# A sixteen-batch two-layer transformer block: the rows for the second layer's experts written before the second head group's copy and turned later, and VectorE's loop closed before the second normalisation

## The chip, the cores and the metric

The kernel runs on one core of a Trainium2 chip. The metric is the device time of one execution in microseconds. Before the change it was 1889.29 us, the median of 3 runs (1885.23 to 1890.84).

## What is computed

The input is 16 sequences of 512 tokens with 128 features. Four residual steps follow, the first three behind a layer normalisation without weights:

```
x = x + attention_0(layernorm(x))   # 16 heads of 8; q and k scaled to length 1; no softmax; (k'v) first
x = x + experts_0(layernorm(x))     # 8 experts, top 2 by softmax score, and 2 shared ones; silu(x w1) * (x w3) @ w2
x = x + attention_1(layernorm(x))   # 16 heads of 8, softmax with a causal band mask
x = x + experts_1(layernorm(x))     # 16 experts; each takes the 512 tokens with the highest logits, gelu between two layers
```

For the last line a token is normalised once more inside the experts' layer: `xn = xf / rms(xf) * norm_weight`, the router's logits are `xn @ router_weight.T + router_bias`, and each expert gathers the rows `xn[idx]` that it takes. So each batch has to leave behind, besides its x, its 512 normalised rows (called `row` in the kernel) and their logits. The experts themselves run after the sixteenth batch.

## The kernel before, in words

**Stages of a batch.** The kernel keeps several batches in flight. Each batch passes a front stage f (first attention, first experts), a stage r (q, k and v of the second attention, split into bf16 parts and sent through DRAM into the tiles `QT` and `KT`), a stage b (the second attention's scores, row maxima, exponentials and products) and a tail stage t (output projection, x3, `row`, router). Work alternates between two phases, written once and run by all engines in the same order, each engine with its own instruction queue:

- `x_phase(f, b, t, g)`: the first experts of batch f (ten units: `up`, `up3`, `product`, `down`), beside them the scores by query of batch b, whose row maxima VectorE takes (`maxima`), and the start of batch g;
- `y_phase(b, f, r, t)`: the scores by key of batch b, whose exponentials ScalarE takes (`exps`), the products with v in four head groups (`outputs(0)` to `outputs(3)`), beside them the first attention of batch f (`f_kvq`, `f_kv`, `f_kvo`, `f_out`, `f_turn_x1`, `f_gate`), stage r of another batch, and the tail of batch t.

The order inside a phase is written out by hand for each engine. Engines meet only through semaphores. `looped` (line 268) runs five phases as straight code, then a loop over i from 1 to BATCH - 3 with an x_phase and a y_phase in its body, then six more phases as straight code. TensorE, ScalarE and POOL close their loop between a y_phase and the next x_phase.

**The scores.** A batch has 40 fills (`scores`) of three PSUM banks `ba`, in each phase once. In a y_phase fill n waits for exponential n - 3, and `outputs(k)` (line 834) waits for exponentials 0 to 10k + 9 and, for k > 0, for the normalisation `norm(k - 1)`. Each head group goes the same way: `outputs(k)` on TensorE into the bank `bo`, a copy `oT<-bo` on VectorE (also called `outputs`, line 1377), `turn_outputs(k)` on TensorE back into `bo` (line 743), `norm(k)` on VectorE (lines 1269 and 1271: a reciprocal `rden`, and the product into `ao`). Only then may the next group's products be written to `bo`.

**VectorE in a y_phase.** The order before the change is: `r_norm`, `f_bias`, `r_center`, `f_bias`, `f_l2`, `r_rest`, `f_scale`, `outputs(0)`, `r_rest`, `t_stats`, `norm(0)`, `f_kvm`, `t_square`, `outputs(1)`, `t_row`, `norm(1)`, `f_x1`, `outputs(2)`, `t_logits`. Then follow, in a second part called with `rest=True`, `norm(2)`, `f_logits`, `f_gates`, `f_rank` and `outputs(3)`. VectorE's loop is closed between the two parts: its body is the rest of a y_phase, an x_phase, and the first part of the next y_phase. `fc`, `mc`, `rc` and `tc` are counters of the steps of one batch; `fc.b` tells the counter which batch it is in.

**The rows of the second experts.** `t_stats` takes mean and variance of x3; POOL raises to the power -0.5 (`power`, line 452, `t_rs`); `t_square` makes from it the variance of the normalised rows (`t_ve`), POOL takes a second power (`t_rs2`); `t_row` multiplies the two (`t_sc`, line 1300) and writes `row` with four instructions (line 1146). TensorE's `t_turn_row` turns `row` into `facc` (line 729, four transposes), ScalarE copies that with the norm's weight into `rowT` (line 1043), and TensorE's `t_router` (line 735) makes the logits, which VectorE's `t_logits` stores (line 1307). SyncE sends `row` to DRAM (`row_dmas`, line 347), behind the transfers of the next `QT` and `KT` of the first eight heads.

**The front's side.** `f_kvo` (line 642) makes k'v times the output weights in `fa[1]`, ScalarE copies it into `kvo` behind exponential 24, `f_out` (line 648) makes the attention's output, and `f_x1` on VectorE (from line 1209) adds it to x, takes the statistics, waits for a power of POOL (`f_rs`) and writes `f_n`, which `f_turn_x1` turns (line 609).

Of the kernel before, what the change touches and what calls it, by code (L numbers as in the profile page):

```python
# [20 lines left out]
BATCH, SEQ, D = 16, 512, 128  # L21
# [24 lines left out]
def build_kernel(nc, a, out):  # L46
    ctx = ExitStack()
    with ctx:
# [557 lines left out]
        def _(pe):  # L606
# [202 lines left out]
            def y_phase(b, f, r, t):  # L809
                def fills(*ns):  # L810
                    if b is None:
                        return
                    for n in ns:
                        if n == 0:
                            pe.wait_ge(S["s_mx0"], 16 * PARTS * (b + 1))
                            pe.wait_ge(S["s_red"], FILLS * (b + 1))
                        if n == FILLS // 2:
                            pe.wait_ge(S["s_mx1"], 16 * PARTS * (b + 1))
                        if n >= 3:
                            pe.wait_ge(S["s_exp"], FILLS * b + n - 2)  # L820
                        scores(pe, b, n, True)

                def outputs(k, *beside):
                    if b is None:
                        return
                    pe.wait_ge(S["s_exp"], FILLS * b + 10 * k + 10)
                    if k == 0:
                        pe.wait_ge(S["s_nmT"], 2 * b + 2)
                    else:
                        pe.wait_ge(S["s_norm"], 4 * b + k)  # L830

                    for blk in range(Q):
                        for j in range(4):
                            last = pe.matmul(bo[32 * j:32 * j + 32, blk * P:], lhsT=vp[:, blk, 4 * k + j],  # L834
                                             rhs=prob_block(4 * k + j, blk), start=blk == 0, stop=blk == Q - 1)
                        if blk == Q - 1:
                            last.then_inc(S["s_pv"], 1)
                        fills(*beside[blk:blk + 1])

                def if_b(step, *args):  # L840
                    if b is not None:
                        step(b, *args)

                def if_f(step, *args):
                    if f is not None:
                        step(f, *args)

                def if_r(step):
                    if r is not None:
                        step(r)  # L850

                def if_t(step, *args):
                    if t is not None:
                        step(t, *args)

                if_f(f_kvq, 0)
                fills(0, 1, 2)
                if_f(f_kvq, 1)
                fills(3, 4)
                if_b(turn_maxima, 1)  # L860
                if_r(r_turn)
                fills(5, 6, 7)
                if_r(r_q)
                fills(8, 9, 10, 11)
                outputs(0, 12, 13, 14)
                if_r(r_k)
                fills(15, 16, 17)
                if_b(turn_outputs, 0)
                fills(18, 19)
                if_f(f_kv)  # L870
                fills(20, 21)
                outputs(1, 22, 23, 24)
                if_f(f_kvo)
                if_t(t_turn_row, r)
                fills(25, 26, 27)
                if_b(turn_outputs, 1)
                fills(28, 29)
                if_f(f_out)
                fills(30, 31)
                outputs(2, 32, 33, 34)  # L880
                if_t(t_router)
                fills(35, 36)
                if_f(f_turn_x1)
                fills(37)
                if_b(turn_outputs, 2)
                fills(38, 39)
                if_f(f_gate)
                if r is not None:
                    if t is not None:
                        pe.wait_ge(S["s_l1c"], t + 1)  # L890
                    r_v(r)
                outputs(3)
# [73 lines left out]
        def _(act):  # L966
# [37 lines left out]
            def y_phase(b, f, r, t):  # L1004
                def exps(first, last):
                    if b is None:
                        return
                    for n in range(first, last + 1):
                        pair, f_ = divmod(n, 5)
                        act.wait_ge(S["s_st"], FILLS * b + n + 1)  # L1010
                        if f_ == 0:
                            act.wait_ge(S["s_pv"], 4 * b + max(pair - 1, 0) // 2)
                        act.activation(probs[:, pair % 3, f_], ba[n % 3][:], ACT.Exp, scale=SCALE).then_inc(S["s_exp"], 1)  # L1013

                if b is not None:
                    act.activation(warm[:], m_b[:, 0:1], ACT.Exp, scale=0.0)
                exps(0, 4)
                if b is not None:
                    copy(nmT[:, 1], bo[:].bitcast(BF16)[0:PARTS * HEADS // 2, 0:SEQ], "s_nmt", 2 * b + 2, "s_nmT")
                if r is not None:  # L1020
                    copy(b_nT[:], facc[:], "s_T3", r + 1, "s_nT3")
                exps(5, 5)
                if f is not None:
                    act.wait_ge(S["s_kvqe"], Q * f + Q)
                    act.activation(sq[:].rearrange("p q (w d) -> p q w d", w=2), kvq[:].rearrange("p q (w d) -> p q w d", w=3)[:, :, 0:3:2],
                                   ACT.Square).then_inc(S["s_sq"], 1)
                exps(6, 7)
                if r is not None:
                    act.wait_ge(S["s_qkw"], 48 * r)
                    copy(qkp[:, 0, 0], facc[:], "s_q", r + 1, "s_p1")  # L1030
                exps(8, 14)
                if r is not None:
                    copy(qkp[:, 1, 0], facc[:], "s_k", r + 1, "s_p1")
                exps(15, 19)
                if f is not None:
                    copy(qnT[:], fa[0][:], "s_qT", f + 1, "s_qnT")
                exps(20, 24)
                if f is not None:
                    copy(kvo[:], fa[1][:, 0:D], "s_kvo", f + 1, "s_kvoc")
                exps(25, 26)  # L1040
                if t is not None:
                    act.wait_ge(S["s_T4"], t + 1)
                    act.activation(rowT[:], facc[:], ACT.Copy, scale=norm_col[:]).then_inc(S["s_nT4"], 1)
                exps(27, 36)
                if f is not None:
                    copy(f_nT[:], fa[0][:], "s_T2", f + 1, "s_nT2")
                exps(37, 39)
                if f is not None:
                    act.wait_ge(S["s_lgx"], f + 1)
                    act.activation(sc[:], lg[:], ACT.Exp).then_inc(S["s_exf"], 1)  # L1050
                if r is not None:
                    act.wait_ge(S["s_pv"], 4 * r)
                    copy(vp[:, :, :, 0:HD], facc[:].rearrange("p (q h d) -> p q h d", q=Q, h=HEADS), "s_v", r + 1, "s_vp")
# [41 lines left out]
        def _(dve):  # L1095
# [283 lines left out]
            def y_phase(b, f, r, t, rest=False):  # L1379
                def if_b(step, k):  # L1380
                    if b is not None:
                        step(b, k)

                def if_f(step, *w):
                    if f is not None:
                        step(f, *w)
# [5 lines left out]
                def if_t(step):  # L1392
                    if t is not None:
                        step(t)

                if rest:
                    fc.b = f
                    if_b(norm, 2)
                    if_f(f_logits)
                    if_f(f_gates)  # L1400
                    if_f(f_rank)
                    if_b(outputs, 3)
                    return
# [10 lines left out]
                if_b(norm, 0)  # L1414
                if_f(f_kvm)
                if_t(t_square)
                if_b(outputs, 1)
                if_t(t_row)
                if_b(norm, 1)
                if_f(f_x1)  # L1420
                if_b(outputs, 2)
                if_t(t_logits)

            def y_whole(b, f, r, t):
                y_phase(b, f, r, t)
                y_phase(b, f, r, t, True)
# [3 lines left out]
            x_phase(0, None, None, 1)  # L1430
            y_whole(None, 1, 0, None)
            x_phase(1, 0, None, 2)
            y_phase(0, 2, 1, None)
            with dve.Fori(1, BATCH - 2) as i:
                y_phase(i - 1, i + 1, i, i - 2, True)
                x_phase(i + 1, i, i - 1, i + 2)
                y_phase(i, i + 2, i + 1, i - 1)
# [221 lines left out]
```

## Time and profile before

| | |
|---|---|
| median of 3 runs | 1889.29 us (1885.23 to 1890.84) |
| the profiled execution: its time | 1888.15 us |
| its span in the profile | 1885.8 us |
| mean granted clock of TensorE over the span | 0.907 |
| first and last turn of `row` | 268.13 and 1522.9 us |
| passes of VectorE's loop | 13 |
| after the batches: choice of tokens and the sixteen experts | from about 1527 us |

The profile is one execution. Times are microseconds from the start of the span. PE is TensorE's matmuls, PEld its weight loads, DVE VectorE, ACT ScalarE, POOL GpSimd, SP SyncE. A timeline's line gives the start, the time from the first start to the last end of the merged instructions, the engine, the line of the kernel, the operation with its output and inputs, the number of instructions and, in square brackets, how long the engine sat idle before it and what released it. "Issue" as a releaser says that the engine waited for nothing that the profile shows. The granted clock of TensorE has two levels, 1.00 (2.4 GHz) and 0.50 (1.2 GHz); a number in between is the mean of a stretch that has both.

### The profile page before, as it was taken

To read this page: it belongs to the slowest core of one execution; us is meant where nothing else is said; L and a number is where in the kernel's file an instruction comes from. 1 tells how busy PE (TensorE), PEld (TensorE's weight loads), DVE (VectorE), ACT (ScalarE), POOL (GpSimd) and SP (SyncE) were. 2 spreads that over 40 slices of the span, in tenths; PEclk is the share of its full clock that TensorE was granted. 3 is DMA by queue.
4 is the path that set the end of the run, shared out by engine and by line. 5 is a ranking of instruction groups with operands and counts; after the bars stand their busy time and mean duration, and the time that the engine had idled before them with its cause. 6 is when DMAs were issued, how large, how long until landed. Compare 5 with 4: busy or idle time off the path is not lost.

```text
span 1885.8 us, 35247 instructions
## 1 busy us (share of the span) xinstructions
PE 1558.1 (83%) x10840; PEld 974.4 (52%) x10840; DVE 1217.5 (65%) x3591; ACT 862.5 (46%) x1787; POOL 518.3 (27%) x498
## 2 busy tenths in 40 slices
PE   2889989999999999998989898999998821356765
PEld 2455656565655555565656565656564411244654
DVE  5567868686868686867777686868675358821110
ACT  1436464645555554545464646464553412423331
POOL 1322222131313131312222222213121020038886
PEclk7879999999999999999999999999999765578897
DMA  2031121303030303031221212130303000034443
GB/s 70 1 79 47 40 64 29 73 18 85 7 84 7 84 15 81 24 67 39 52 54 37 54 37 58 33 77 14 79 8 84 8 12 0 1 73 95 91 85 60
DMA packets 83244, 90.77 MB, mean 48 GB/s; under 512 B 19520, under 2 KB 73024, under 8 KB 78528
## 3 DMA queue, kind: packets, MB, share of 16 engines
q1 hardware_dynamic: 71872, 80.76, 17.5%
q0 software_dynamic: 11264, 8.92, 3.5%
q14 instruction: 84, 0.69, 0.1%
q8 instruction: 24, 0.39, 0.1%
HBM read 58.95 MB, written 29.92 MB: 47 GB/s over the span
## 4 chain that ended last, share of the span: by engine, by line
PE 52%; DVE 18%; issue 15%; POOL 6%; DMA 3%; ACT 3%; SPq 1%; DVEq 1%; POOLq 0%; ACTq 0%
PE fa L675 7%; PE ba L585 6%; PE ba L580 6%; PE fa L667 6%; PE bo L834 5%; PE fa L685 4%; POOL out L552 3%; PE ba L587 2%; PE facc L685 2%; PE ba L953 2%; DVE passed L1488 2%; PE ba L582 2%; DVE nm L1258 2%; DMA QT<-nmT 2%; POOL got L522 2%
## 5 line engine op out<-in xcount | busy, mean ns | idle before, releaser
L1013 ACT ACTIVATE probs<-ba 128x512 f32<-128x512 f32 x640 | 352.3, 598 | 191.9 <-PE ba L582 190.7
L458 POOL TENSOR_TENSOR x<-x,gd 128x512 f32<-128x512 f32 x144 | 182.5, 1267 | 615.4 <-ACT gd L991 598.1
L580 PE MATMUL ba<-QT,KT 75*128 75x512 bf16 (+3 forms) x1024 | 262.2, 319 | 27.7 <-ACT probs L1013 14.5
L585 PE MATMUL ba<-KT,QT 72*128 72x512 bf16 (+3 forms) x1024 | 244.2, 305 | 7.4 <-DVE nm L1258 3.2
L580 PEld LDWEIGHTS ba<-QT,KT 75*128 75x128 bf16 x1024 | 106.7, 104 | 188.0 <-ACT probs L1013 104.1
L582 PE MATMUL ba<-mask_k,identb 128*128 128x128 bf16 x1024 | 200.2, 229 | 0.0
L1258 DVE TENSOR_REDUCE nm<-ba 128x1 f32<-128x512 f32 x256 | 174.3, 681 | 36.0 <-PE ba L587 36.0
L587 PE MATMUL ba<-mask_q,identb 128*128 128x128 bf16 x1024 | 192.9, 222 | 0.0
L834 PE MATMUL bo<-probs,vp 128*32 128x512 f32 (+3 forms) x2048 | 182.2, 445 | 1.7 <-ACT probs L1013 0.9
L675 PE MATMUL fa<-f_nT,w 128*128 128x512 f32 x320 | 174.3, 627 | 2.5 <-DVE hh L1250 1.5
L667 PE MATMUL fa<-f_nT,w 128*128 128x512 f32 x320 | 173.8, 625 | 0.0
L585 PEld LDWEIGHTS ba<-KT,QT 72*128 72x128 bf16 x1024 | 101.2, 99 | 99.6 <-issue 37.6
L1260 DVE TENSOR_REDUCE nm<-ba 128x1 f32<-128x384 f32 x256 | 140.3, 548 | 16.6 <-PE ba L587 16.6
L991 ACT ACTIVATE gd<-facc,gates 128x128 f32<-128x128 f32 x256 | 73.2, 369 | 131.0 <-PE facc L685 131.0
L984 ACT ACTIVATE sil<-fa 128x512 f32<-128x512 f32 x160 | 95.3, 596 | 76.9 <-PE fa L667 76.9
L587 PEld LDWEIGHTS ba<-mask_q,identb 128*128 128x128 bf16 x1024 | 101.8, 99 | 55.1 <-issue 53.6
L1250 DVE TENSOR_TENSOR hh<-sil,fa 128x512 f32<-128x512 f32 x160 | 108.6, 678 | 15.5 <-PE fa L685 8.8
L991 ACT ACTIVATE gd<-fa,gates 128x128 f32<-128x128 f32 x256 | 73.2, 369 | 92.4 <-PE fa L685 92.4
L582 PEld LDWEIGHTS ba<-mask_k,identb 128*128 128x128 bf16 x1024 | 105.8, 103 | 15.6 <-issue 13.1
L552 POOL DMA_INDIRECT out<-contrib,cur x64 | 100.7, 1574 | 30.8 <-issue 18.6
L1596 DVE TENSOR_TENSOR ysum<-ba,fb 128x512 f32<-128x512 f32 x16 | 11.1, 691 | 151.6 <-PE ba L953 151.6
L1377 DVE COPY oT<-bo 128x512 f32<-128x512 f32 x64 | 44.1, 690 | 88.2 <-PE bo L834 88.2
(279 smaller groups left out, 2785.1 us busy)
## 6 DMA issues: line engine op xcount, KB each, us to landing
QT<-qk_parts SPq DMA_DIRECT2D x96, 192.0 KB
KT<-qk_parts SPq DMA_DIRECT2D x96, 192.0 KB
qk_parts<-qkp SPq DMA_DIRECT2D x32, 384.0 KB, 2.5
fc<-in_L_ffn_fc_weight SPq DMA_DIRECT2D x32, 256.0 KB, 3.1
xin<-in_L_attn_x SPq DMA_DIRECT2D x16, 256.0 KB, 7.8
qk_parts<-qkp SPq DMA_DIRECT2D x16, 256.0 KB, 2.7
out<-x SPq DMA_DIRECT2D x16, 256.0 KB, 2.3
xn_rows<-row SPq DMA_DIRECT2D x16, 256.0 KB, 6.6
```

Source lines behind the costliest of these rows:

```text
L458: pool.tensor_tensor(x1[:], x1[:], gd[:, e % 2], ALU.add).then_inc(S["s_x1g"], 1)
L552: pool.indirect_dma_start(out_rows, bass.IndirectOffsetOnAxis(cur[k][:, c:c + 1], 0), contrib[k % 2][:, c], None, compute_op=ALU.add).then ...
L580: pe.matmul(bank[:, col:col + w], lhsT=KT[0:K_ROWS, head, blk * P:(blk + 1) * P], rhs=QT[0:K_ROWS, head, blk * P:], start=True, stop=False)
L582: last = pe.matmul(bank[:, col:col + P], lhsT=identb[:], rhs=mask_k[:], start=False, stop=True)
L585: pe.matmul(bank[:, col:col + w], lhsT=QT[0:QK_ROWS, head, blk * P:(blk + 1) * P], rhs=KT[0:QK_ROWS, head, 0:w], start=True, stop=False)
L587: last = pe.matmul(bank[:, col + w - P:col + w], lhsT=identb[:], rhs=mask_q[:], start=False, stop=True)
L667: pe.matmul(fa[0][:], lhsT=w1[:, e], rhs=f_nT[:], start=True, stop=True).then_inc(S["s_h1"], 1)
L675: pe.matmul(fa[1][:], lhsT=w3[:, e], rhs=f_nT[:], start=True, stop=True).then_inc(S["s_h3"], 1)
L834: last = pe.matmul(bo[32 * j:32 * j + 32, blk * P:], lhsT=vp[:, blk, 4 * k + j], rhs=prob_block(4 * k + j, blk), start=blk == 0, stop=blk ...
L991: last = act.activation(gd[:, e % 2, q], down_bank(e - 2)[:, q * D:(q + 1) * D], ACT.Copy, scale=gates[:, q, e - 2:e - 1])
L1013: act.activation(probs[:, pair % 3, f_], ba[n % 3][:], ACT.Exp, scale=SCALE).then_inc(S["s_exp"], 1)
L1258: last = dve.tensor_reduce(nm[:, 3, h:h + 1], bank[:], X, ALU.max, negate=True)
```

## The change

On TensorE `t_turn_row` moves from behind `f_kvo` to behind fill 29; `f_out` moves from behind fill 29 to behind fill 28. On ScalarE the copy `rowT` moves from behind exponential 26 to behind exponential 29. On VectorE `t_row` moves ahead of `outputs(1)`, and the loop is closed behind `outputs(1)`: `norm(1)`, `f_x1`, `outputs(2)` and `t_logits` go to the part that begins the loop's body. Since that part now has a tail step, which has no batch in the loop's first pass, this pass is written out ahead of the loop, and VectorE's loop runs from 2.

```
@@ TensorE, y_phase
                 if_f(f_kvo)
-                if_t(t_turn_row, r)
                 fills(25, 26, 27)
                 if_b(turn_outputs, 1)
-                fills(28, 29)
+                fills(28)
                 if_f(f_out)
+                fills(29)
+                if_t(t_turn_row, r)
                 fills(30, 31)
                 outputs(2, 32, 33, 34)
                 if_t(t_router)
@@ ScalarE, y_phase
-                exps(25, 26)
+                exps(25, 29)
                 if t is not None:
                     act.wait_ge(S["s_T4"], t + 1)
                     act.activation(rowT[:], facc[:], ACT.Copy, scale=norm_col[:]).then_inc(S["s_nT4"], 1)
-                exps(27, 36)
+                exps(30, 36)
@@ VectorE, y_phase
                 if rest:
                     fc.b = f
+                    if_b(norm, 1)
+                    if_f(f_x1)
+                    if_b(outputs, 2)
+                    if_t(t_logits)
                     if_b(norm, 2)
                     if_f(f_logits)
                     if_f(f_gates)
...
                 if_t(t_square)
+                if_t(t_row)
                 if_b(outputs, 1)
-                if_t(t_row)
-                if_b(norm, 1)
-                if_f(f_x1)
-                if_b(outputs, 2)
-                if_t(t_logits)
@@ VectorE, the phases
             x_phase(1, 0, None, 2)
-            y_phase(0, 2, 1, None)
-            with dve.Fori(1, BATCH - 2) as i:
+            y_whole(0, 2, 1, None)
+            x_phase(2, 1, 0, 3)
+            y_phase(1, 3, 2, 0)
+            with dve.Fori(2, BATCH - 2) as i:
                 y_phase(i - 1, i + 1, i, i - 2, True)
                 x_phase(i + 1, i, i - 1, i + 2)
                 y_phase(i, i + 2, i + 1, i - 1)
```

## Rows read from the trace of the kernel before

**Rows 1.** The page: busy time by engine, and the chain that ended last.

```profile
PE 1558.1 (83%) x10840; PEld 974.4 (52%) x10840; DVE 1217.5 (65%) x3591; ACT 862.5 (46%) x1787; POOL 518.3 (27%) x498
...
PE 52%; DVE 18%; issue 15%; POOL 6%; DMA 3%; ACT 3%; SPq 1%; DVEq 1%; POOLq 0%; ACTq 0%
```

**Rows 2.** The list of waits, 600 to 950: us in total, times, longest.

```profile
PE facc L729 <- DVE row L1146: 7.4, 4, 1.8
...
PE bo L743 <- DVE oT L1377: 3.4, 8, 0.6
```

**Rows 3.** Timeline of PE, one y_phase of the loop.

```profile
265.80 0.49 PE L642 MATMUL fa<-w_o,kvm 128*128 128x128 f32 x2
268.13 0.65 PE L729 MATMUL facc<-ident,row 128*128 128x128 f32 x4 [1.84 <-DVE row L1146]
...
270.66 1.11 PE L648 MATMUL fa<-kvo,qnT 128*128 128x128 f32 x8
271.61 0.38 PE L580 MATMUL ba<-QT,KT 75*128 75x512 bf16 x1
...
272.35 1.06 PE L834 MATMUL bo<-probs,vp 128*32 128x512 f32 x8
...
277.85 0.60 PE L609 MATMUL fa<-ident,f_n 128*128 128x128 f32 x4
...
287.07 0.65 PE L743 MATMUL bo<-ident,oT 128*128 128x128 f32 x4 [0.54 <-DVE oT L1377]
```

**Rows 4.** Timeline of DVE, the same y_phase.

```profile
262.77 0.17 DVE L1296 TENSOR_SCALAR t_ve<-t_ve 128x4 f32<-128x4 f32 x1
265.93 0.69 DVE L1377 COPY oT<-bo 128x512 f32<-128x512 f32 x1 [3.00 <-PE bo L834]
...
266.89 1.11 DVE L1146 TENSOR_SCALAR row<-x,t_mv,t_sc 128x128 f32 x4 [0.19 <-DVE t_sc L1300]
...
271.81 0.69 DVE L1209 TENSOR_TENSOR x<-fa,xres 128x512 f32<-128x512 f32 x1 [1.07 <-PE fa L648]
...
275.36 1.11 DVE L1146 TENSOR_SCALAR f_n<-x,f_mv,f_rs 128x128 f32<-128x128 f32 x4 [1.12 <-POOL f_rs L452]
```

**Rows 5.** Timeline of POOL, the same y_phase: the second power.

```profile
263.02 1.01 POOL L452 TENSOR_TENSOR t_rs<-t_ve,mhalf 128x4 f32<-128x4 f32 x1 [0.82 <-DVE t_ve L1296]
```

**Rows 6.** Windows: busy PE, PEld, DVE, ACT, POOL (instructions); PEclk, DMA share, GB/s.

```profile
266.00:281.00 15.00, 13.16 (x126) 9.03 (x126) 6.64 (x25) 9.37 (x19) 1.01 (x1) 1.00 0.42 95
...
712.00:714.00 2.00, 0.51 (x6) 0.30 (x2) 1.65 (x6) 0.65 (x2) 0.00 (x0) 1.00 0.75 197
714.00:721.00 7.00, 6.65 (x33) 5.46 (x34) 0.77 (x3) 3.42 (x6) 0.00 (x0) 0.51 0.71 150
721.00:728.00 7.00, 7.00 (x71) 3.70 (x70) 4.10 (x16) 3.80 (x7) 1.01 (x1) 1.00 0.00 1
```

**Rows 7.** Line 729 on PE: starts of later turns, and idle before all.

```profile
356.02 1.11 PE L729 MATMUL facc<-ident,row 128*128 128x128 f32 x4 [1.83 <-DVE row L1146]
...
1341.85 0.85 PE L729 MATMUL facc<-ident,row 128*128 128x128 f32 x4 [1.84 <-DVE row L1146]
...
DVE row L1146: 35.0, 16
```

**Rows 8.** Line 1269 (norm) on DVE: behind the loop's end, and over all.

```profile
280.85 0.26 DVE L1269 RECIPROCAL rden<-bo 128x16 f32<-128x16 f32 x1 [3.09 <-issue]
...
L1269 DVE RECIPROCAL rden<-bo x64: 242/256/259, 175.4 to 1512.9; 128x16 f32<-128x16 f32 x64
...
issue: 34.5, 12
```

**Rows 9.** Timeline of ACT, the same y_phase: the exponentials behind `kvo`.

```profile
269.17 1.09 ACT L1013 ACTIVATE probs<-ba 128x512 f32<-128x512 f32 x2 [2.57 <-PE ba L582]
```

**Rows 10.** DMA by queue: 726.5 to 730, then 730 to 732: packets, MB, share.

```profile
q14 instruction: 1, 0.01, 0.8%
...
q14 instruction: 1, 0.01, 3.1%
```

More of the change, by code:

```diff
@@ L873, in y_phase @@
                 if_f(f_kvo)
-                if_t(t_turn_row, r)
                 fills(25, 26, 27)
                 if_b(turn_outputs, 1)
-                fills(28, 29)
+                fills(28)
                 if_f(f_out)
+                fills(29)
+                if_t(t_turn_row, r)
                 fills(30, 31)
@@ L1039, in y_phase @@
                     copy(kvo[:], fa[1][:, 0:D], "s_kvo", f + 1, "s_kvoc")
-                exps(25, 26)
+                exps(25, 29)
                 if t is not None:
@@ L1043, in y_phase @@
                     act.activation(rowT[:], facc[:], ACT.Copy, scale=norm_col[:]).then_inc(S["s_nT4"], 1)
-                exps(27, 36)
+                exps(30, 36)
                 if f is not None:
@@ L1397, in y_phase @@
                     fc.b = f
+                    if_b(norm, 1)
+                    if_f(f_x1)
+                    if_b(outputs, 2)
+                    if_t(t_logits)
                     if_b(norm, 2)
@@ L1416, in y_phase @@
                 if_t(t_square)
+                if_t(t_row)
                 if_b(outputs, 1)
[L1418 to L1422, printed above, removed]
             def y_whole(b, f, r, t):
@@ L1432, in _ @@
             x_phase(1, 0, None, 2)
-            y_phase(0, 2, 1, None)
-            with dve.Fori(1, BATCH - 2) as i:
+            y_whole(0, 2, 1, None)
+            x_phase(2, 1, 0, 3)
+            y_phase(1, 3, 2, 0)
+            with dve.Fori(2, BATCH - 2) as i:
                 y_phase(i - 1, i + 1, i, i - 2, True)
```

## Prediction, made before the change was run

> **What bounds the kernel now.** I read the busy shares first [rows 1]: TensorE is busy 83% of the span, VectorE 65%, ScalarE 46%, and the chain that ended last is 52% TensorE. So up to about 1,527 us, while the batches pass, time is gained only where TensorE idles or runs slowly. The list of waits over four passes of the loop says where it idles on VectorE: 1.8 us per pass before line 729, the turn of `row`, and 3.4 us in 8 times, 0.6 at most, before line 743, the turns of the outputs [rows 2].
>
> The reader is then to look at one second phase (y_phase) at full clock [rows 3]. TensorE starts `f_kvo` at 265.80 and then idles 1.84 us before the turn of `row` at 268.13; nothing else of the group waits. On VectorE [rows 4] the last thing that `t_row` needs from its own engine, `t_ve`, is done at 262.94, and POOL's power on it took 1.01 us from 263.02 [rows 5]. Then VectorE stands 3.00 us, because `outputs(1)`, the copy of the second head group, is ahead of `t_row` in its queue and waits for TensorE's line 834. Only after that copy come `t_sc` and the four writes of `row`, to 268.00. The stall is made by the order of two steps, not by missing data.
>
> The stall has a second price. From 712 to 714 TensorE worked 0.51 us of 2; from 714 to 721 the granted clock was 0.51, the lower of its two levels (1.2 of 2.4 GHz), and before and after it was 1.00 [rows 6]. The pass of 268 has the same stall and stays at 1.00 [rows 6]. Every later pass of the loop falls, each right behind the stall and nowhere else (windows of 2 us over the loop, of which the group shows one pass). The starts of line 729 price it [rows 7]: from 268.13 to 356.02 is 87.89 us with no fall between; the eleven intervals from 356.02 to 1341.85 last 985.83 us, against 11 x 87.89 = 966.79. So eleven falls cost 19.0 us.
>
> Third, the end of VectorE's loop. Behind `logits` it starts nothing until 280.85, 3.09 us put down to issue; over all passes it is 34.5 us in 12 times, 2.9 each [rows 8]. Behind it `lg`, the gates and the fourth copy are late, and TensorE waits 0.54 us for that copy at 287.07 [rows 3]. Of the 3.4 us of [rows 2], one wait of 0.56 per pass is the first copy's; 3.4 - 4 x 0.56 = 1.2 in four passes, 0.3 each, lies behind the loop end.
>
> **Part 1: `t_row` ahead of `outputs(1)` on VectorE.** Power done at 264.03, `t_sc` at about 264.3, the wait of 0.19 or so and four writes of 1.11 in all: `row` is ready at about 265.7. VectorE was idle there for 3.00 us [rows 4], which hides all of it. The copy starts at 265.93 as before, with a margin of 0.2 us; if a power came late the copy would slip, but TensorE's turn of it comes only after three more score fills, 0.9 us on. SyncE's one DMA of `row` becomes free to leave 2.3 us sooner; it still stands behind the QT/KT transfers in the queue, has the same size, and nothing in the pass reads it: nothing.
>
> **Part 2: the turn moved on TensorE, behind fills 25 to 29 and `f_out`.** The same instructions follow without the hole: what lies between 268.13 and `outputs(2)` at 272.35 [rows 3] is 4.22 us of work and starts at 268.13 - 1.84 = 266.29, so `outputs(2)` starts at 270.5. `f_out` moves ahead of the turn (at most 0.65) and of fill 29 (0.36): it was done at 271.61, 3.48 us after 268.13, and is now at 266.29 + 3.48 - 0.85 = 268.9. ScalarE must keep up: its next exponential came 2.57 us late because of the stall [rows 9]. Now five exponentials at some 0.52 (1.09 for two [rows 9]) from 266.6 end by 269.9 even with gaps, ahead of 270.5 where `outputs(2)` wants them. The `rowT` copy behind them ends near 270.6, and `t_router` comes only after `outputs(2)`. Its move costs nothing.
> Thirteen passes x 1.84 = 23.9 us. The idle before line 729 is 35.0 us in 16 times [rows 7], so the last three turns have 35.0 - 23.9 = 11.1. The very last has no head groups beside it and keeps its wait, the most of these; the other two are like the loop's, though with less work of other stages between the fills, so ScalarE limits sooner. I take 1.6 each, 3.2.
>
> **Part 3: the clock.** With no hole TensorE works on, and the nearest stretch without this stall, 721 to 728 with the same kind of head-group products, has clock 1.00 [rows 6]. The holes of up to 0.6 us before line 743 never brought a fall. So the low stretches go: 19.0 us for eleven and as much again for one, 1.3, behind the stall of 1341.85: 20.3. Bounds: 0, if something else there makes it fall, and 20.3.
>
> **Part 4: the loop end.** Its old place becomes plain code: `norm(2)` and `lg` follow TensorE, and the 0.3 us at the fourth copy goes, 12 x 0.3 = 3.6. Bounds 0 and 12 x 0.54 = 6.5; I take 3.6.
> At the new place, behind the second copy (ends at 266.62 [rows 4]), 2.9 us reach to 269.5; `norm(1)` takes 0.6 and is done at 270.1; `outputs(2)` wants it at 270.5: a margin of 0.4 us, 0.3 with the semaphore's way. `f_x1`, queued behind it, finds `f_out` ready since 268.9. Its chain took 271.81 to 276.47, 4.66 us with POOL's power in it [rows 4], and now ends at 274.8; TensorE wants `f_n` at 277.85 - 272.35 = 5.5 us behind `outputs(2)`'s start [rows 3], at 276.0: a margin of 1.2.
> So the cover is thin and the length of this end decides. It has a fetch in it: in the old, quiet place the one packet of the instruction queue took 0.8% of 16 engines x 3.5 us = 0.45 us; between 730 and 732, in other traffic, one took 3.1% of 16 x 2 us = 1.0 us [rows 10]. The new place lies in traffic, 0.71 to 0.75 of the DMA engines' time [rows 6]. Bounds for the added length: 0 (the same length) and 2 us (this fetch and a following one, each doubled, and queueing); I take the difference of the two packets, 0.55, of which 0.25 shows on TensorE. Eleven ends are left: 2.8 us lost.
> The Trainium skill (Runtime: NRT & Kernel Launch, Instruction fetch mechanics) says that a taken branch to a target outside what the engine holds must wait for a DMA fetch of it. By that rule the end lasts as long as a transfer does and speaks against this new place; the packet inside the gap agrees.
> The peeled pass is straight code; `norm` shows an issue gap only 12 times in 64 [rows 8], one for each loop end, none in the straight passes: nothing.
>
> **The sum.** 23.9 + 3.2 + 20.3 + 3.6 - 2.8 = 48.2 us. The profiled execution took 1888.15 us, 1.1 below the median of 1889.29 of the runs shown; 1888.15 - 48.2 = 1840. Its own range is 1832 (the two upper bounds of part 4 and of the last turns, and some 3 us of low clock in the last passes that may shift) to 1848.
>
> **The rivals.**
> - The stall goes, the clock falls all the same. Against it: no fall anywhere else in the loop. For it: the stretch ahead of the hole is 128x32 products, little work per matmul, and `f_kvo` is small. Then 20.3 stays: 1860. Chance 0.12.
> - The loop end stretches in its new place to 4 to 5 us. At 4.5 `norm(1)` is 1.3 late beyond the margin: 11 x (1.3 - 0.25) = 12, so 1852; were that hole to bring the falls of [rows 7] again, 1866. Chance 0.12.
> - Slower than before, at the same place: VectorE between the second copy and `norm(1)`, with `outputs(2)` and `f_x1` behind it. If the code comes only after the QT/KT and `row` transfers (traffic until 721 in that pass [rows 6]), the end takes 8 us: 11 x 4.8 = 53, and the falls return with so long a hole, 19: 1912. It decides from an end of about 7.5 us with the clock kept (48.2 / 11 = 4.4 beyond the 3.1 to 3.2 that hide), 6 us with the falls. No row shows one beyond 3.1. Chance 0.03.
> - The change does not do what it says: `row` is still last because a power ends late (POOL's queue has the parts of q and k ahead of it). POOL was waiting for `t_ve`, not late [rows 5], so little speaks for it: 1888, chance 0.03.
>
> **The numbers.** The forecast has 0.70, the rivals 0.12, 0.12, 0.03, 0.03. The range 1830 to 1862 holds the forecast, the clock rival and the nearer part of the longer loop end. About 0.3% is what a measurement of this kernel can tell from no change. Faster by more: 0.94; within: 0.03; slower: 0.03.
>
> **What would show it.** Right: no wait of TensorE on `row`; starts of line 729 some 86 us apart (87.89 - 1.84 - 0.3 + 0.25); clock 1.00 through the loop; `norm(2)` waiting for TensorE's turn and not for issue; an issue gap of 3 to 3.5 us before `norm(1)`, with at most 0.3 us on TensorE before `outputs(2)`. Wrong: a new TensorE wait on `ao` at line 834, an issue gap above 4 us, or a clock of 0.5 in passes that have no hole.

## The result, and the profile after

The changed kernel takes 1865.84 us (median of 4 runs, 1860.58 to 1867.44), the kernel before 1887.26 us in the runs beside it. The ratio is 0.9876, with a 95% interval of 0.9857 to 0.9895: 1.2% faster, where 2.5% and 1840 us had been forecast. The profiled execution took 1865.44 us with a span of 1863.5 us. Its time is 22.7 us less than that of the profiled execution before, where the sum said 48.2.

The wait on `row` is gone, and another stands in its place. The list of waits of the changed kernel over the same four passes as [rows 2] (us in total, times, longest):

```profile
DVE rden L1270 <- issue: 21.2, 4, 5.8
...
PE bo L834 <- DVE ao L1272: 9.4, 4, 2.9
...
PE bo L743 <- DVE oT L1378: 3.7, 4, 0.9
```

TensorE used to idle 7.4 us in these passes on `row` and now idles 9.4 us on `ao`, the result of `norm(1)`; behind it VectorE idles 21.2 us in four times for issue alone. (VectorE's lines have moved by one: 1270 is the reciprocal of `norm`, 1269 of before.) One pass shows how. The timeline of VectorE:

```profile
347.99 1.12 DVE L1147 TENSOR_SCALAR row<-x,t_mv,t_sc 128x128 f32 x4 [0.20 <-DVE t_sc L1301]
349.49 0.69 DVE L1378 COPY oT<-bo 128x512 f32<-128x512 f32 x1 [0.38 <-PE bo L834]
355.41 0.26 DVE L1270 RECIPROCAL rden<-bo 128x16 f32<-128x16 f32 x1 [5.23 <-issue]
```

And that of TensorE, without its score fills:

```profile
349.35 0.49 PE L642 MATMUL fa<-w_o,kvm 128*128 128x128 f32 x2
350.57 0.60 PE L743 MATMUL bo<-ident,oT 128*128 128x128 f32 x4
351.35 1.11 PE L648 MATMUL fa<-kvo,qnT 128*128 128x128 f32 x8
352.64 0.60 PE L729 MATMUL facc<-ident,row 128*128 128x128 f32 x4
356.14 1.07 PE L834 MATMUL bo<-probs,vp 128*32 128x512 f32 x8 [2.28 <-DVE ao L1272]
```

`row` is done at 349.11, 0.38 us before the copy can start, and the turn at 352.64 waits for nothing. Without its wait of 2.28 us TensorE would have begun `outputs(2)` at 353.86, 4.5 us behind the start of `f_kvo`; the sum had 4.7. But the loop end, which begins when the copy ends at 350.18, lasts 5.23 us and not the 3.45 of the sum (2.9 + 0.55), and everything behind it is late. Over all passes, the two lines of line 1270's idle time (releaser, us, times) that answer to [rows 8]:

```profile
L1270 DVE RECIPROCAL rden<-bo x64: 244/257/259, 173.8 to 1490.8; 128x16 f32<-128x16 f32 x64
...
issue: 56.7, 11
```

That is 5.15 us per end, where it was 2.9 before. And the hole has taken over the second price too. The windows of the changed kernel (columns as in [rows 6]):

```profile
354.00:356.00 2.00, 0.00 (x0) 0.00 (x0) 0.55 (x3) 0.99 (x3) 0.00 (x0) 1.00 0.75 156
356.00:362.00 6.00, 5.86 (x46) 1.97 (x46) 3.43 (x15) 1.79 (x3) 1.01 (x1) 0.72 0.20 45
362.00:370.00 8.00, 8.00 (x82) 5.74 (x82) 4.45 (x22) 3.96 (x9) 0.00 (x0) 1.00 0.35 84
```

TensorE is at 1.2 GHz for part of the six us behind the hole. Six of the eleven passes with a loop end fall so; before, twelve of thirteen did. The starts of line 729 give the account, since the first pass has no loop end any more. From the timeline of TensorE, three of the sixteen:

```profile
267.12 0.61 PE L729 MATMUL facc<-ident,row 128*128 128x128 f32 x4
352.64 0.60 PE L729 MATMUL facc<-ident,row 128*128 128x128 f32 x4
...
1328.49 0.60 PE L729 MATMUL facc<-ident,row 128*128 128x128 f32 x4
```

From 267.12 to 352.64 are 85.52 us. The eleven intervals behind it last 975.85 us, against 11 x 85.52 = 940.7: 35.1 us too much. The waits of line 834 on `ao` in ten of them are 22.9 us (1.29 to 2.87 each). The eleventh has the same hole, of 1.24 us, under another name:

```profile
1243.68 0.29 DVE L1272 TENSOR_TENSOR ao<-bo,rden 128x128 f32<-128x128 f32 x1
1244.12 1.06 PE L834 MATMUL bo<-probs,vp 128*32 128x512 f32 x8 [1.24 <-ACT probs L1014]
```

The profile names an exponential, but `ao` was done at 1243.97, behind a loop end of 4.20 us, and the pass is 1.3 us longer than the one without a loop end. So 24.1 us are holes. Of the other 11.0 us, 10.5 lie in the six passes at low clock (about 1.6 in five, 2.6 in the sixth).

### The profile page after: what moved, and what is told of

Read it like the earlier page. It is cut to its first block, busy times and chain, and to the rows that moved or that the text cites. A ratio compares the mean times of both kernels' runs of the same rounds, so it can differ in the third digit from the quotient of the medians.

```text
span 1863.5 us, 35097 instructions
## 1 busy us (share of the span) xinstructions
PE 1540.5 (83%) x10840; PEld 958.2 (51%) x10840; DVE 1219.9 (65%) x3591; ACT 859.9 (46%) x1787; POOL 519.0 (28%) x498
## 4 chain that ended last, share of the span: by engine, by line
PE 52%; issue 16%; DVE 16%; POOL 8%; ACT 3%; DMA 3%; SPq 1%; DVEq 1%; POOLq 0%; ACTq 0%
PE fa L675 7%; PE ba L585 6%; PE bo L834 6%; PE fa L667 6%; PE ba L580 5%; POOL out L552 4%; PE fa L685 4%; PE ba L587 3%; PE facc L685 2%; POOL got L522 2%; DVE passed L1491 2%; PE ba L582 2%; DMA QT<-nmT 2%; DVE nm L1259 1%; SPq L341 1%
## 5 line engine op out<-in xcount | busy, mean ns | idle before, releaser
L458 POOL TENSOR_TENSOR x<-x,gd 128x512 f32<-128x512 f32 x144 | 182.7, 1269 | 619.2 <-ACT gd L992 602.0
L580 PE MATMUL ba<-QT,KT 75*128 75x512 bf16 (+3 forms) x1024 | 252.7, 309 | 26.9 <-ACT probs L1014 13.5
L834 PE MATMUL bo<-probs,vp 128*32 128x512 f32 (+3 forms) x2048 | 189.8, 460 | 26.0 <-DVE ao L1272 23.8
L582 PE MATMUL ba<-mask_k,identb 128*128 128x128 bf16 x1024 | 194.1, 224 | 0.0
L1264 DVE TENSOR_REDUCE nm<-ba 128x2 f32<-128x512 f32 x128 | 87.5, 684 | 14.2 <-PE ba L587 12.7
```

The source lines that it names most:

```text
L458: pool.tensor_tensor(x1[:], x1[:], gd[:, e % 2], ALU.add).then_inc(S["s_x1g"], 1)
L580: pe.matmul(bank[:, col:col + w], lhsT=KT[0:K_ROWS, head, blk * P:(blk + 1) * P], rhs=QT[0:K_ROWS, head, blk * P:], start=True, stop=False)
L582: last = pe.matmul(bank[:, col:col + P], lhsT=identb[:], rhs=mask_k[:], start=False, stop=True)
```

## The experiments

All are edits of one of the two kernels. In all but the last the loop end is measured by VectorE's idle time for issue before the reciprocal of `norm`. Three readings were on trial: T, the loop end is long in its new place because its code fetch meets the transfers; R1, its length depends on where the loop's code lies; R2, the clock falls in this part of a pass whatever TensorE does.

### The other half: the loop end left where it was

```
# from the kernel before; TensorE and ScalarE as changed, VectorE untouched
-                if_t(t_turn_row, r)
                 fills(25, 26, 27)
                 if_b(turn_outputs, 1)
-                fills(28, 29)
+                fills(28)
                 if_f(f_out)
+                fills(29)
+                if_t(t_turn_row, r)
@@ ScalarE
-                exps(25, 26)
+                exps(25, 29)
...
-                exps(27, 36)
+                exps(30, 36)
```

> TensorE's and ScalarE's part alone; VectorE as before (t_row behind outputs(1), loop closed behind t_logits). Theory T (the loop end is long in its new place because its code fetch meets the QT/KT transfers; everything else of the forecast holds): VectorE's row is ready at 268.0 in the pass of 268, the turn comes only at 269.2, so no wait on row, no clock falls in the loop, loop end 2.8 to 3.1 us as before. Time 1841 us, 1836 to 1846; starts of line 729 about 86 us apart. Rival R1 (the length of the end depends on where the loop's code lies, not on traffic): the same. Rival R2 (the clock falls in this part of a pass whatever TensorE's hole): falls stay, 1860.

1830.46 us (1830.14 to 1832.72), 0.9692 of the kernel before (0.9667 to 0.9718): 35 us better than the whole change. TensorE's starts of line 729, the first and the thirteenth, and VectorE's idle before line 1270:

```profile
267.80 0.61 PE L729 MATMUL facc<-ident,row 128*128 128x128 f32 x4
...
1293.87 0.61 PE L729 MATMUL facc<-ident,row 128*128 128x128 f32 x4
```

```profile
issue: 33.9, 12
```

Twelve passes of 85.51 us, and a granted clock of 1.00 from 350 to 1350 (the windows view's line for that stretch):

```profile
350.00:1350.00 1000.00, 962.66 (x7188) 590.32 (x7184) 783.10 (x2337) 544.94 (x1180) 245.36 (x219) 1.00 0.21 50
```

R2 falls: with no hole above 0.7 us the clock does not fall once in the loop, so the falls were the stall's doing. The time lies below the range expected (1836 to 1846).

The same with `t_row` ahead of the copy, so the whole change but for the loop end:

```
# added to the edit above
+                if_t(t_row)
                 if_b(outputs, 1)
-                if_t(t_row)
```

> The whole change except the loop end: TensorE's and ScalarE's order and t_row ahead of outputs(1), but VectorE's loop closed behind t_logits as before. T (the end costs its time only in the traffic of its new place): 1830 us, 1827 to 1834, equal to TensorE's part alone; loop end 2.8 to 3.0 us; no falls in the loop, passes 85.5 us apart. R1 (place of the code): 1830 only if the end is short by luck; a gap of 4 us or more there would be for it. That t_row's move matters by itself would show as a difference from 1830.5 of more than 4 us.

1833.91 us (1833.05 to 1834.11), 12 passes of 85.60 us, loop ends of 34.7 us in 12. `t_row`'s move is worth nothing when TensorE's turn is late enough: in the run above, where `row` is written at its old place, it is done at 266.72 and the turn starts at 267.80. Of the 3.7 us between the spans of the two profiled executions, 1.6 lie ahead of the loop (the first turn of `row` starts at 269.38, not 267.80) and 1.1 in its twelve passes.

### VectorE's part alone

```
# from the changed kernel; TensorE and ScalarE as before
+                if_t(t_turn_row, r)
                 fills(25, 26, 27)
                 if_b(turn_outputs, 1)
-                fills(28)
+                fills(28, 29)
                 if_f(f_out)
-                fills(29)
-                if_t(t_turn_row, r)
```

> VectorE's part of the change alone; TensorE turns row right behind f_kvo and ScalarE copies rowT behind exponential 26, as before. T: row is ready at about 265.7, before f_kvo ends, so no wait on row; the loop end is as long as in the changed kernel (4.2 to 5.8 us), so the wait on ao and some falls stay: 1866 us, 1860 to 1872. If TensorE's move had been needed, a wait on row would be left and the time above 1872.

1866.57 us (1864.49 to 1873.15), 0.9871 (0.9847 to 0.9895): the changed kernel's time. Its loop ends are 56.9 us in 11, its waits on `ao` 1.28 to 2.53 us. So either of the two moves of `row`, the writing earlier or the turning later, takes the stall away; the loop end costs the same beside each.

### The loop end alone

```
# from the kernel before: VectorE's loop closed behind outputs(1) and t_row; its first pass written out as in the change
                     fc.b = f
+                    if_b(norm, 1)
+                    if_f(f_x1)
+                    if_b(outputs, 2)
+                    if_t(t_logits)
                     if_b(norm, 2)
...
                 if_t(t_row)
-                if_b(norm, 1)
-                if_f(f_x1)
-                if_b(outputs, 2)
-                if_t(t_logits)
```

> The kernel before with the loop end alone moved to behind outputs(1) and t_row; TensorE still stalls on row. T: the end begins at 268.0 in the pass of 268, 1.4 us later than in the changed kernel, lasts about 5, so norm(1) ends near 273.6 and outputs(2) starts 1.3 us late in eleven passes, with longer low clock behind: 1905 us, 1895 to 1925, slower than before. R1: with a gap of 3 us nothing is late and the time is 1887, minus a few us for the old place.

1897.86 us (10 runs, 1893.11 to 1902.60), ratio 1.0044 (1.0030 to 1.0059): slower than before, though less than expected. The loop end behind `row` in one pass, and all of them:

```profile
360.97 0.26 DVE L1269 RECIPROCAL rden<-bo 128x16 f32<-128x16 f32 x1 [6.41 <-issue]
```

```profile
issue: 68.3, 11
```

6.2 us each. In this pass it begins 3.1 us behind the issue of the first QT/KT transfer, in the changed kernel's 1.7 us, so 1.4 us deeper in them, and it is longer still.

### The transfers taken away from the loop end

```
# from the changed kernel; SyncE, in its loop
                 part_dmas(i + 1)
+                sp.wait_ge(S["s_norm"], 4 * i + 2)
                 back_dmas(i + 1, 0)
                 row_dmas(i - 1)
```

> The changed kernel, but SyncE sends the first half of QT and KT (and so row) only after norm(1) of the pass, so no transfer runs during the loop end. T: the issue gap before norm(1) shrinks from 4.2 to 5.8 us to about 3, TensorE's wait on ao before outputs(2) and the falls go: 1840 us, 1835 to 1848, unless the later half of the transfers makes the first fill of the x_phase wait. R1: the gap stays at 5 us and the time at 1866.

1830.11 us (1828.86 to 1832.32), 0.9688 (0.9662 to 0.9715). VectorE's program is that of the changed kernel; only SyncE waits. One loop end, and all:

```profile
354.36 0.26 DVE L1271 RECIPROCAL rden<-bo 128x16 f32<-128x16 f32 x1 [2.41 <-issue]
```

```profile
issue: 25.9, 11
```

2.4 us each, from 5.15; no wait on `ao` in the loop, no falls. This is the decisive run for T. The packets of the instruction queue (q14) say where the time goes; the view does not name the engine they are for, but each of the loop ends here has exactly one. First the changed kernel, the queues' lines from 350.2 to 352.9 and from 352.9 to 355.4 (packets, MB, share of 16 engines); its loop end runs from 350.18 to 355.41:

```profile
q1 hardware_dynamic: 165, 0.53, 85.1%
...
q1 hardware_dynamic: 129, 0.41, 80.9%
q14 instruction: 1, 0.01, 1.5%
```

Then the held kernel, 352 to 354.4, of a loop end that runs from 351.95 to 354.36:

```profile
q14 instruction: 1, 0.01, 1.1%
```

The one packet of code lasts 1.5% x 16 x 2.5 = 0.6 us in traffic and 1.1% x 16 x 2.4 = 0.4 us without. That difference is small. What is long is the time until it starts: in the changed kernel's pass there is none in the first 2.6 us of the end. Windows of 0.2 us over all eleven ends give the same: the packet is recorded 1.8 to 3.4 us into the end in the changed kernel, 0.2 to 0.8 us into it with the transfers held. Behind it VectorE goes on after some 2.2 to 2.7 us and some 1.9 to 2.1 us. How the queued transfers hold the packet back is not shown.

### Only half of the traffic

```
# from the changed kernel, SyncE: QT/KT alone across the end
                 back_dmas(i + 1, 0)
-                row_dmas(i - 1)
                 back_dmas(i + 1, 1)
+                row_dmas(i - 1)
# from the changed kernel, SyncE: row alone across the end
                 part_dmas(i + 1)
+                row_dmas(i - 1)
+                sp.wait_ge(S["s_norm"], 4 * i + 2)
                 back_dmas(i + 1, 0)
-                row_dmas(i - 1)
                 back_dmas(i + 1, 1)
```

> The changed kernel with the DMA of row sent behind the second half of QT and KT instead of between the halves, so that only the six QT/KT transfers, already queued when the loop end begins, run across it. Theory TQ (the queued QT/KT transfers delay the code fetch): gap before norm(1) stays at 4 us or more, TensorE keeps its wait on ao, 1858 us or more. Rival TR (row's 512 small packets do it): gap about 3 us, time near 1833.

> The changed kernel with QT and KT held until norm(1) as in e4, but row sent at once, so that row's transfer alone runs across the loop end. TQ: gap below 3 us, 1830 to 1834. TR: gap 4 us or more and 1858 us or more. Both at work: gap 3 to 4, and little of it shows.

With the QT/KT transfers alone across the end the time is 1856.21 us (1852.01 to 1869.79), with `row`'s transfer alone 1829.14 us (1828.35 to 1831.36). The idle time for issue of the one, then of the other:

```profile
issue: 52.5, 11
```

```profile
issue: 31.5, 11
```

4.8 us per end with QT/KT, 2.9 with `row`, 2.4 with neither, 5.15 with both. The six QT/KT transfers do most of it, `row`'s half a us. (The first of the two missed its bound by 2 us in the time, not in the gap.)

### The same code in another place

```
# from the changed kernel; VectorE, ahead of its first wait for the weights
+            for _ in range(128):
+                apart(dve)
```

> The changed kernel with 128 empty instructions in VectorE's stream before its first wait on the weights, so that the loop's code lies elsewhere and nothing else is different. T: gap before norm(1) 4.2 to 5.8 us as in the changed kernel, time 1866 within 4. R1: the gap changes by more than 1 us in either direction and the time by 10 us or more.

1863.03 us (1861.46 to 1866.53):

```profile
issue: 56.0, 11
```

5.1 us per end: moved by 128 empty instructions (`apart` issues one), the code takes as long. R1 falls for this shift; other shifts were not tried.

### The transfers laid on the old loop end

```
# from the kernel with TensorE's part alone; SyncE, in its loop
                 part_dmas(i + 1)
+                sp.wait_ge(S["s_l1"], 1 * i)
                 back_dmas(i + 1, 0)
```

> TensorE's part alone (1830.5 us, loop end 2.8 to 3.0 us) with the first half of QT and KT held back until t_router is done, so that these transfers now run across the old loop end. T: the gap before norm(2) grows from 2.8 to between 4 and 6 us in the same code at the same place of the loop; TensorE waits for ao before outputs(3) and perhaps for the transfers before the first fill: 1845 us or more. R1: the gap stays at 2.8 to 3.0 and only waits for the transfers are added.

1919.50 us (1917.25 to 1921.58), ratio 1.0152 to the kernel before. Most of the 89 us above TensorE's part alone is another wait, 4.7 us a pass for the late KT before the first fill of the x_phase. The loop ends:

```profile
issue: 40.9, 12
```

```profile
278.81 0.26 DVE L1271 RECIPROCAL rden<-bo 128x16 f32<-128x16 f32 x1 [3.16 <-issue]
```

3.4 us each, from 2.8: the direction T wants, but less than expected (4 to 6). SyncE's queue in that pass, and the packets of 275.7 to 278.8, suggest why:

```profile
275.51 0.36 SPq L333 DMA_DIRECT2D QT<-qk_parts  x1
275.96 0.33 SPq L333 DMA_DIRECT2D KT<-qk_parts  x1
276.39 0.31 SPq L333 DMA_DIRECT2D QT<-qk_parts  x1
```

```profile
q1 hardware_dynamic: 70, 0.43, 58.1%
q14 instruction: 1, 0.01, 2.2%
```

The loop end began at 275.66, with one transfer issued. In the changed kernel's pass it is four of the six, with the loop end alone all six. The packet comes 0.8 to 1.0 us into the end, as it does in the quiet old place, but it lasts 2.2% x 16 x 3.1 = 1.1 us. So with one transfer issued the packet starts on time and is only stretched. With four it starts 2.6 us into the end, and with six 3.8 us. That what is already queued counts, and not the share of traffic in the stretch (58% here, 81 to 85% in the changed kernel), is likely from this series, but the two were not separated.

### A loop end ahead of the QT and KT transfers

```
# from the changed kernel; the loop closed behind t_square, ahead of the copy
                     fc.b = f
+                    tc.b = t
+                    if_b(outputs, 1)
+                    if_t(t_row)
                     if_b(norm, 1)
...
                 if_t(t_square)
-                if_t(t_row)
-                if_b(outputs, 1)
```

> The changed kernel with the loop closed one step earlier, behind t_square and ahead of outputs(1), where VectorE waits for TensorE anyway and the QT/KT transfers have not begun; t_row goes behind the copy again. T: gap 3 us or so, covered by the 3.0 us VectorE waits there; no wait on row (ready at 268.4, wanted at 269.2), none on ao: 1838 us, 1833 to 1845, faster than the changed kernel by 1.5%. R1: the gap is whatever the code's place makes it; if 5 us, the copy is 2 us late and the time about 1865.

1833.10 us (1831.49 to 1834.19), 0.9702 (0.9676 to 0.9727). The profile puts the wait of the copy behind the loop end down to TensorE:

```profile
351.16 0.69 DVE L1378 COPY oT<-bo 128x512 f32<-128x512 f32 x1 [3.43 <-PE bo L834]
```

That hides most of this end, not all. With TensorE's part alone, where no loop end stands here, the same wait is 3.00 us and the copy starts 0.49 us behind the start of the last products (line 834); here it starts 0.92 us behind it. So the end itself lasts 3.4 us and makes the copy 0.4 us late, which costs a pass 0.1 us (85.64 us against 85.51). Nor is it ahead of all traffic: from 347.7 to 349.1 the DMA engines are still busy with SyncE's writes of `qk_parts`, and the code's packet is recorded 1.4 to 1.6 us into each of the eleven ends, when they are over. That is T once more, with other transfers.

The kernels whose loop end is covered or has no QT/KT transfers across it all lie at 1829 to 1834 us, 1.7 to 2.0% under the changed kernel. `row` sent at once and QT and KT held (1829.14) is the lowest; TensorE's part alone (1830.46) is the least edit and as good within the spread of the runs.

## Why the prediction was wrong

**What failed** is a term of the sum in its part 4, the loop end in its new place. The mechanism was there, as a cost and as a rival: the end fetches code, the new place lies in the QT/KT transfers, and the cover is 0.3 us. The size was not. "I take the difference of the two packets, 0.55, of which 0.25 shows on TensorE" gave 2.8 us; the end grew by 2.3 us (5.15 against 2.9), past the upper bound of 2, and cost 35.1 us, 24.1 in holes and 11.0 behind them, nearly all at low clock. The error was to price the fetch by the duration of its packet. That grows by 0.2 us only; the wait for its start grows most (from some 0.4 us into the end to some 2.6, held against changed), and no row of before held it, since the one packet seen in traffic was not one that VectorE stood waiting for. The stretched end was given 0.12. That its price of 1866 us, with the falls, is the measured time is luck: it had holes of 12 us where 24.1 were measured, it added 14 us for the falls where the 19.0 of [rows 7] would have given 1871, and the pass itself turned out shorter than counted. The range left it out in any case.

**Part 1** was right: `row` at 0.38 us ahead of the copy (0.2 forecast), the copy not late. That it is not needed beside part 2 was not seen.

**Part 2** was right: no wait on `row`, `outputs(2)` wanted 4.5 us behind `f_kvo` (4.7), ScalarE not in the way.

**Part 3** was right in its rule, shown by five kernels with no hole above 0.93 us and no fall in the loop (TensorE's part, with `row` first, held, `row` alone, the end ahead of QT and KT). It was overrun in the changed kernel because the new hole is about as long as the old.

**The old place of the end** was put at 3.6 us and is worth nothing in the pass. The wait before the fourth copy's turn did go; but the wait before the first copy's turn grew from 0.56 us to 0.9, and the passes are 85.51 us long with the end in its old place (TensorE's part) and in the new one (held). What was won at the head of the x_phase was given back at the first copy. Why the copy does not come earlier was not followed.

**The rest.** A pass without a hole is 85.5 us, where 87.89 - 1.84 = 86.05, less 0.3 for the old place of the end, was counted: 0.25 us a pass better, 3 in all, and its cause is not settled. Taking out the 35.1 us, the changed kernel gained 57.4 us of span (22.3 + 35.1) where the sum had 51.0 (48.2 + 2.8). Besides these 3 us the difference lies behind the loop, where 8.9 us were gained and 4.5 counted (ahead of it 1.0 and 1.8). Low-clock stretches shift there; which of them made the difference was not followed.

**The rivals.** The clock that falls all the same: refuted. A late power: refuted, POOL was in time. Slower than before: not the change. Its place was right, and the loop end alone (1.0044) is slower; but the code did not wait for all the transfers: its packet comes at 352.8 and they last until about 358. The Trainium skill's rule (Runtime: NRT & Kernel Launch, Instruction fetch mechanics), that a taken branch to code not at hand waits for a DMA fetch, is borne out: each end has one packet of the instruction queue, and it takes 2.4 us with the transfers held and 5.15 with them, in the same VectorE program.

## What to carry to other kernels

The end of VectorE's loop is here a transfer's wait (the lists of waits show no such gap for the matmuls of TensorE or for ScalarE, whose loops end elsewhere). Look for such a gap in the profile, put it where that engine waits anyway and where no large transfers are already queued, and price it by a whole issue gap seen in such traffic, not by the duration of its packet. When an engine stalls on something that another writes too late, look first whether the reader can come later; here TensorE's part alone gave all of the gain. And a stall of TensorE costs more than its length, because the clock may fall behind it; so a change that moves a hole instead of closing it wins little.

## What the runs showed of the hardware

- A hole of about 2 us can bring TensorE's clock to 1.2 GHz, but not each time: of holes of 1.84 us twelve in thirteen did (kernel before); in the changed kernel six of eleven of 1.24 to 2.87 us, while holes of 2.54, 2.60 and 2.62 us did not. A pass with a fall was 1.2 to 2.9 us longer than its hole explains.
- The same loop end of VectorE, in the same program, takes 2.3 to 2.5 us with idle DMA queues and 4.2 to 5.8 us amid six transfers of 192 KB, four of them issued before it begins, and `row`'s behind them; the end that begins 1.4 us further into them, with all six issued, takes 5.4 to 6.7 us. The code's packet is recorded 0.2 to 0.8 us into the end in the quiet case and 1.8 to 3.4 us into it in the busy one. In another quiet place (the old one) the end takes 2.8 to 3.1 us with the packet at 0.8 to 1.2 us; why that place is longer was not followed.
- One transfer of 256 KB from another tile (`row`), alone across the end, added 0.5 us.
